# Two transformer-like layers on one core: one opening block with the loads that the first attention needs, the rest loaded and made during that attention

## What is computed

```
ga = (2 * (ga >= 0) - 1) * max(|ga|, 0.25)          # gb alike
h = layernorm(x) * (1 + ca) + sa ;  x = x + ga * attn(h)
h = layernorm(x) * (1 + cb) + sb ;  x = x + gb * ffn(h)
```

## Time and profile before

| | us |
|---|---|
| three runs | 4078.65, 4080.57, 4083.61 |
| median | 4080.57 |
| the profiled execution | 4077.96 |
| its span in the trace | 4076.2 |

### The profile page before, as it was taken

How to read it: one execution, slowest core, us unless ns; L and a number is a source line. 1 busy time by engine, 2 the same in 40 slices (tenths; PEclk the granted TensorE clock), 3 DMA queues, 4 the chain that set the end, 5 groups by cost and what they waited for, 6 DMA issues and landing times. The chain is left out here.

```text
span 4076.2 us, 49893 instructions
## 1 busy us (share of the span) xinstructions
PE 3502.1 (86%) x16757; PEld 2034.7 (50%) x16757; DVE 3318.9 (81%) x3665; ACT 2577.2 (63%) x3716; POOL 2721.2 (67%) x1957
## 2 busy tenths in 40 slices
PE   5488888989898998989897898989889898989876
PEld 3154553637355463736455373645546373644522
DVE  3513687989888898989887898988989898988997
ACT  2345666766676766766676676666667676667652
POOL 0031676958677685968766695877768696776892
PEclk9599999999999999999999999999999999999888
DMA  3520110303021020302112030301103030211100
GB/s 136 183 88 32 58 63 8 118 1 109 16 67 59 28 98 6 116 4 91 35 53 74 6 119 1 99 27 57 69 21 104 1 109 16 78 47 42 68 1 11
DMA packets 66249, 236.01 MB, mean 58 GB/s; under 512 B 9120, under 2 KB 9760, under 8 KB 65568
## 3 DMA queue, kind: packets, MB, share of 16 engines
q1 hardware_dynamic: 63648, 223.81, 16.3%
q10 hardware_dynamic: 2304, 8.39, 0.5%
HBM read 212.25 MB, written 19.92 MB: 57 GB/s over the span
## 5 line engine op out<-in xcount | busy, mean ns | idle before, releaser
L672 POOL TENSOR_TENSOR kept<-kept,hb 128x512 f32<-128x512 f32 x600 | 757.5, 1294 | 20.2 <-DVE hb L1989 19.6
L1980 DVE TENSOR_TENSOR_SCAN hb<-ps,hb 128x512 f32<-128x512 f32 x600 | 697.8, 1206 | 17.7 <-ACT ps L1404 13.1
L938 PE MATMUL ps<-hid_bhi,wring 128*128 128x512 f32 x1408 | 560.9, 398 | 16.0 <-DVE ln_s L2007 16.0
L938 PE MATMUL ps<-hid_blo,wring 128*128 128x512 f32 x1408 | 554.1, 394 | 0.0
L1404 ACT ACTIVATE ps<-kept,a_neg 128x512 f32<-128x512 f32 x600 | 403.3, 695 | 188.1 <-DVE hb L1980 188.1
L938 PE MATMUL ps<-hid_ahi,wring 128*128 128x512 f32 x1280 | 515.2, 402 | 4.9 <-DVE h_ln L2007 4.4
L633 POOL TENSOR_SCALAR_AFFINE_SELECT room<-room 128x512 f32<-128x512 f32 x256 | 224.3, 893 | 431.3 <-ACT room L1628 429.4
L938 PE MATMUL ps<-hid_alo,wring 128*128 128x512 f32 x1280 | 505.0, 395 | 0.0
L2055 DVE TENSOR_REDUCE room<-ps 128x4 f32<-128x2048 f32 (+3 forms) x256 | 375.1, 1486 | 118.1 <-PE ps L1132 118.1
L640 POOL TENSOR_TENSOR kept<-kept,hb 128x1024 f32<-128x1024 f32 x112 | 288.9, 2590 | 249.0 <-DVE hb L1924 181.1
L1628 ACT ACTIVATE room<-ps 128x2048 f32<-128x2048 f32 (+1 forms) x192 | 305.3, 1590 | 205.4 <-PE ps L1158 178.5
(11 more groups left out here) (319 smaller groups left out, 7680.1 us busy)
## 6 DMA issues: line engine op xcount, KB each, us to landing
wring<-w_hi SPq DMA_DIRECT2D x352, 512.0 KB, 3.3
kept<-in_wffn SPq DMA_DIRECT2D x22, 512.0 KB, 4.4
w_hi<-wring SPq DMA_DIRECT2D x22, 512.0 KB, 3.6
xn<-in_x_fm SPq DMA_DIRECT2D x17, 512.0 KB, 3.2
out_fm<-xc ACTq DMA_DIRECT2D x15, 512.0 KB, 2.7
room<-in_wmod SPq DMA_DIRECT2D x2, 1536.0 KB, 7.8
win<-in_win SPq DMA_DIRECT2D x1, 1024.0 KB, 8.7
wqk<-in_wqk SPq DMA_DIRECT2D x1, 512.0 KB, 5.7
```

What stands on the lines that cost most here:

```text
L672: pool.tensor_tensor(acc[:, m, :], acc[:, m, :], hb[:, s % 8, :], ALU.add).then_inc(acc_done, 1)
L938: mm = pe.matmul(bank(bk), w, x, start=(k == 0 and i == 0), stop=(k == K - 1 and i == 1))
L1980: dve.tensor_tensor_scan(hb[:, s % 8, :], bank(2 + m % 2), hb[:, s % 8, :], 0.0, ALU.mult, ALU.add).then_inc(scanned, 1)
```

## The change

The set-up block, the two small blocks and the layernorm pass become one block, `opening`. It issues 16 loads (both `c`, `mean_mat`, `x`, `wmod0`, and eleven more that the attention needs), has a semaphore for each of four groups of loads, and makes only layer 0's modulation, in the middle of which PE does the variance. The other 14 loads (3.9 MB; `wmod1` of 1536 KB, `win` of 1024 KB, `wout` of 512 KB, `ffw`, `wxp` and `wdt` of 256 KB each, and eight of 32 KB or less) are issued by SP in the first attention, one behind the load of each of the tiles 3 to 16. Layer 1's modulation and the state-space constants are made late in the first attention (`later_pe` behind `row_sums(1)`, `later_act` before `exp_probs(3, 1)`, `later_dve` behind `weigh(2)`). The rounding of the feed-forward weight goes to the start of the feed pass on DVE, its transposes and its copy to the end of that pass on PE and ACT. The calls `split` move two tiles ahead on ACT and DVE: tiles 0 and 1 come before the attention's first instruction, and each later place takes a tile two numbers higher.

```diff
-        with nc.Block() as block:
-            n_set = len(SETUP_LOADS) + 10
...
+        LATER = [(wxp, "wxp"), (wdt, "wdt"), (win, "win"), (s1, "s1"), (s2, "s2"), (sh1, "sh1"), (sh2, "sh2"),
+                 (ffb, "ffb"), (bdt_neg, "bdt"), (d_skip, "d_skip"), (wout, "wout")]
+        N_LATER = len(LATER) + 3
...
+        LATER_LOADS = [(wm[1], "wmod1"), (a_rows(), "a_log"), (ffw.rearrange("p a b -> p (a b)"), "ffw")] + [(whole(t), name) for t, name in LATER]
+
+        def modulation(pe, i, m, bk):
+            for c in range(DC):
+                mm = pe.matmul(bank(bk)[:, m * B:(m + 1) * B], wm[i][:, c, m * P:(m + 1) * P],
+                               c_s[:, i, c * B:(c + 1) * B], start=(c == 0), stop=(c == DC - 1))
+            return mm
...
+        def opening():
+            n_opening = 11
+            with nc.Block() as block:
+                @block.sync
+                def _(sp):
+                    sp.dma_start(c_in[:, 0, :], a["c0"]).then_inc(c_loaded, 16)
+                    sp.dma_start(c_in[:, 1, :], a["c1"]).then_inc(c_loaded, 16)
+                    sp.dma_start(whole(mean_mat), a["mean_mat"]).then_inc(x_loaded, 16)
+                    sp.dma_start(xn[:, :, :], a["x_fm"][0]).then_inc(x_loaded, 16)
+                    sp.dma_start(wm[0], a["wmod0"]).then_inc(mod_loaded, 16)
...
+                @block.scalar
+                def _(act):
+                    act.wait_ge(c_loaded, 32)
+                    act.activation(c_s, c_in, ACT.Silu).then_inc(set_act, 1)
+                    act.preload_act_table_set(LN_EXP)
+                    act.wait_ge(next_cent, 1)
+                    act.activation(qk_sq, ln_x[:, :, :], ACT.Square).then_inc(next_sq, 1)
+                    act.wait_ge(next_var_done, 1)
...
+                    act.wait_ge(set_pe, 1)
+                    copy_modulation(act, 0, 0)
+                    act.wait_ge(next_norm, 1)
+                    act.wait_ge(set_dve, 2)
...
+                @block.tensor
+                def _(pe):
+                    pe.wait_ge(x_loaded, 32)
+                    for c in range(DC):
+                        mm = pe.matmul(bank(6), mean_mat[:, :], xn[:, c, :], start=(c == 0), stop=(c == DC - 1))
+                    mm.then_inc(next_mean_done, 1)
+                    pe.wait_ge(mod_loaded, 16)
+                    pe.wait_ge(set_act, 1)
+                    for m in range(6 * DC):
+                        mm = modulation(pe, 0, m, 0)
+                        if m == 3:
+                            pe.wait_ge(next_sq, 1)
+                            for c in range(DC):
+                                vv = pe.matmul(bank(7), mean_mat[:, :], qk_sq[:, c, :], start=(c == 0), stop=(c == DC - 1))
+                            vv.then_inc(next_var_done, 1)
+                    mm.then_inc(set_pe, 1)
...
+                @block.vector
+                def _(dve):
+                    dve.wait_ge(next_mean_done, 1)
+                    dve.tensor_tensor(ln_x[:, :, :], xn[:, :, :], bcast_c(bank(6)), ALU.subtract).then_inc(next_cent, 1)
+                    dve.wait_ge(next_rstd_ready, 1)
+                    dve.tensor_tensor(ln_x[:, :, :], ln_x[:, :, :], bcast_c(bank(7)), ALU.mult).then_inc(next_norm, 1)
+                    dve.wait_ge(set_act, 2)
+                    scales_of(dve, 0)
+                    gates_of(dve, 0, 2)
+                    dve.wait_ge(loaded, 16 * n_opening)
...
+        def later_pe(pe):
+            pe.wait_ge(loaded, 16 * N_LATER)
+            for m in range(6 * DC):
+                mm = modulation(pe, 1, m, 5)
+            mm.then_inc(set_pe, 1)
+        def later_act(act):
+            act.wait_ge(loaded, 16 * N_LATER)
+            act.activation(a_rows(), a_rows(), ACT.Exp).then_inc(set_act, 1)
+            act.wait_ge(set_pe, 1)
+            copy_modulation(act, 1, 5)
+        def later_dve(dve):
+            dve.wait_ge(set_act, 2)
+            scales_of(dve, 1)
+            gates_of(dve, 1, 2)
...
+        def feed_dve(dve):
+            for i in range(QN):
+                quant(dve, ffw, DC * D // QB, set_dve, 12, i)
+        def feed_pe(pe):
+            pe.wait_ge(set_dve, 12 + QN)
...
                     sp.dma_start(stage[:, t % 3, :], a["wffn"][t]).then_inc(stage_loaded[t % 3], 16)
+                    if 3 <= t < 3 + N_LATER:
+                        to, name = LATER_LOADS[t - 3]
+                        sp.dma_start(to, a[name]).then_inc(loaded, 16)
...
             row_sums(1)
+            if first:
+                later_pe(pe)
             head_spread(0, 1)
...
+            split(0, 1)
             square(0)
...
             odd_version(0)
-            split(0)
+            split(2)
...
+            split(0, 1)
+            if ffn and not att:
+                feed_dve(dve)
             normalise(0)
...
         has_rest = None
-        run([Pass(-1, False, False, False, False, True, False, ())])
+        opening()
         turn_over()
```

More of the change, by code:

```diff
@@ L296, in quant @@
             ins.then_inc(own, 1)
-        c_t = part(REST + 0, DC, B)
-        c_s = part(REST + 64, 2, DC * B)
-        wm = [part(REST + 2560 + i * DC * 6 * D, DC, 6 * D) for i in range(2)]
         c_in = part(REST + 128, 2, DC * B)
-        a_log = part(REST + 256, IM * NS)
+        c_s = part(6144, 2, DC * B)
+        wm = [part(REST + 2560, DC, 6 * D), part(3072, DC, 6 * D)]
+        tmp_g = part(6208, 2 * 2 * DC * B)
         qk_in = part(REST + 384, 4)
@@ L307, in build @@
         grp = part(REST + 400, DC * 2 * D // HS)
-        ffw = part(REST + 1024, DC * D // QB, QB)
-        tmp_g = part(REST + 1536, 2 * 2 * DC * B)
         sel_in = part(REST + 2048, 2 * NS)
-        SETUP_LOADS = [(ident, "ident"), (mean_mat, "mean_mat"), (head_mat, "head_mat"), (sum_sel, "sum_sel"), (wqk, "wqk"), (wv, "wv"), (wu, "wu"),
-                       (win, "win"), (wxp, "wxp"), (wdt, "wdt"), (wout, "wout"), (s1, "s1"), (s2, "s2"), (sh1, "sh1"),
-                       (sh2, "sh2"), (s3, "s3"), (ffb, "ffb"), (bdt_neg, "bdt"), (d_skip, "d_skip")]
+        ffw = b_rows.rearrange("p a b -> p (a b)")[:, 0:DC * D].rearrange("p (a b) -> p a b", b=QB)
@@ new lines, in feed_dve, with feed_act @@
+        def feed_dve(dve):
[3 more added lines that the diff above has]
+            pe.wait_ge(set_dve, 12 + QN)
+            rows = ffw.rearrange("p a b -> p (a b)")
+            for r in range(DC):
+                for c in range(DC):
+                    mm = pe.transpose(bank(2)[:, c * D + r * P:c * D + (r + 1) * P], rows[:, r * D + c * P:r * D + (c + 1) * P], ident[:, :])
+            mm.then_inc(set_pe, 1)
+        def feed_act(act):
+            act.wait_ge(set_pe, 2)
+            act.activation(wdq[:, :, :], bank(2).rearrange("p (c n) -> p c n", c=DC), ACT.Copy).then_inc(set_act, 1)
@@ L1754, in scalar_pass @@
             exp_probs(2, 0)
-            split(21)
             skip(2)
@@ L1770, in scalar_pass @@
             copy_out(2)
+            if first:
+                later_act(act)
             exp_probs(3, 1)
@@ L1859, in scalar_pass @@
             rotate_b()
+            if ffn and not att:
+                feed_act(act)
         def vector_pass(dve, p):
@@ L2123, in vector_pass @@
             find_max(0, 1)
-            split(1)
+            split(3)
             normalise(3)
-            split(2)
+            split(4)
             tail_out(0, 0)
@@ L2189, in vector_pass @@
             weigh(2)
+            if first:
+                later_dve(dve)
             quant_at(1, 4, 5, 6, 7, 8, 9, 10, 11)
```

216 lines of the change are left out of this document (91 added, 125 removed).

## The result

The changed kernel takes 4058.67 us (median of five runs, 4055.03 to 4060.87) against 4079.28 for the kernel before (five runs on the same chip, 4078.65 to 4083.61): a ratio of 0.9947, interval 0.9933 to 0.9960. The forecast was 4064.5, range 4051 to 4073. The profiled execution after took 4057.48, span 4055.7: 20.5 us less than the one before, where the sum of the terms had said 16.2.

What follows compares the result with a forecast made beforehand. Chains bound the opening, a load-rounding-subtraction loop the first attention, later its dependences. Terms -35.7 + 1.0 - 0.3 + 2.0 + 9.5 + 0.3 + 7.0 = -16.2 us took the profiled 4077.96 to 4061.8, written 4064.5 as median; range 4051 to 4073.

Steps and rivals of the forecast that it cites:

- The opening: Set-up to the first attention: one block ends at 29.0 us instead of 64.74, -35.7 us, within 2 us either way.
- the rival's price of 6.3: Fast clock: PE goes fast behind the opening's mean and holds; opening 6.3 us better, total 4052.5; chance 0.21.
- Early tiles and loads: First attention: two tiles split ahead cost +1.0 us (0 to 1.8), later loads in SP's queue +2.0 (0 to 4.1).
- The rival of a loop that pays for every load: First attention: each of 14 loads holds the next tile back 3.5 us, 49 us instead of 2.0; 4111; chance 0.05.
- nothing hidden: Whole change: all moved work may stand on the path, 34.1 against 35.7 us, so -1.6, 4079; chance 0.09.
- The later modulation: Attention's tail on PE: 48 instructions of 8.6 us, 1.3 of it free, plus 2.2 for slower products: +9.5 us.
- The middle case: Later modulation: a third of its instructions fast, the rest slow, +9.5 us; 3.9 if the clock holds, 14 if all slow.
- The feed: Start of the feed pass: rounding delays DVE's centring, +5.2 us, and slows PE's variance, +1.8; together +7.0 (5.2 to 8).

Runs made afterwards that it cites:

- mod_in_gap: Changed kernel with layer 1's modulation on PE moved from the attention's tail to behind `scores_turned(0, 0)`, `wmod1` with its own semaphore: 4048.54 us, ratio 0.9923.
- mod_twice: Changed kernel with layer 1's modulation issued twice in the attention's tail, 96 instructions instead of 48: 4070.25 us in one run.
- both_in_gap: Changed kernel with layer 1's modulation behind `scores_turned(0, 0)` and the feed-forward rounding behind `split(6, 7, 8)`: 4046.49 us, ratio 0.9913.
- before_both: Kernel before with the splits two tiles ahead and the 14 loads issued once more in the first attention: 4080.77 us in one run.

## Why the prediction was right

**The opening** came out term by term: block end 28.8 (forecast 29.0), variance at 13.09 (12.9, where the terms 9.3 + 3.4 give 12.7), the 32 instructions at 0.214 us each. What held the kernel before, the landing of every load, then one engine at a time, was read rightly off.

**But it is not the only opening that occurs.** The forecast argued from 20 us at the slow pace that the clock would not rise, and gave the rise to a rival. Seven of the experiments ran the changed opening or a reordered one with nothing ahead of the mean; with the changed kernel that is eight traces. PE stayed slow to the end of the modulation in three, was fast for the last 32 instructions in three (3.99 to 4.05 us), and rose within the mean or right behind it in two. In these five the first DMA went out 2.7 to 4.9 us earlier than in the changed kernel's trace, more than the 2 us that the forecast allowed the opening; that the trace of the changed kernel is one of the three is luck. So that step of the argument failed: the row it rests on holds where the modulation is PE's first work, in five of five traces, and not behind a mean. The Trainium skill's page "TensorE: Matmul & The Clock Gate" (section "Part 1: The HAM clock gate") says that the point of the rise differs from run to run of one kernel; these traces agree. The Trainium skill's general rule there, that sustained matmul activity releases the throttle, fails at the kernel before: 20.6 us of the modulation never did.

It matters less than the rival's price of 6.3. In the traces whose first DMA went out 2.7 to 2.9 us earlier than after with the same loads (mod_in_gap, mod_twice, both_in_gap) the first exponential came at 82.63, 81.85 and 81.63, against 82.34 and 81.78 in the two with a slow opening. In those three the clock was back at 0.50 in the attention's products 28 to 40 us behind the first DMA, DVE's maxima and the measures of tiles behind them came later, and with them the loads: the one that goes out 40.5 us behind the first DMA in the changed kernel went out at 41.5 to 41.7. Most of the gain was given back, in mod_twice too, which differs from the changed kernel by nothing up to there. This chain is read from the traces; no run set the clock to try it.

**Early tiles and loads.** The two terms, 1.0 and 2.0, measured about 1 at the attention's start and 0.5 to 2 at the first exponential, but they do not simply add up there: the trace pair shows +1.2 for both, against the second trace of the kernel before it is nothing, and before_both, at a lower clock, shows 2.0 and 3.2 against the two. So 3.0 was within what occurs and too much for the profiled execution; that its slow first products hid the early tiles is part of the reason, the rest is open. The rival of a loop that pays for every load (49 us) is out: 14 loads in the kernel before left its end where it was, 4078.49. So is "nothing hidden".

**The later modulation.** +9.5 was forecast and +9.1 measured, out of two errors that cancel: its length was 6.37 and not 8.6, because the clock held for the first 4.3 us of it, and the slow tail behind it cost some 4 and not 2.2 (9.1 less 6.37 - 1.3). The middle case was the right one: the clock fell inside the block, 2.6 to 4.3 us behind its start in all five traces that have it there; in eight of the nine without it the clock stayed at 1.00 for 13 us or more behind the start of `row_sums(1)`. Where the 48 stand there once they took 6.37 to 7.87 us, and the stretch 35.3 each time. The first trace of the kernel before was a short one in this stretch, 26.3 where seven other tails without the modulation took 27.9 and one 29.7; against the seven the modulation cost 7.4, and moving it gave 7.5 there and 8.5 at the end.

**The feed.** +7.0 against +6.9: 5.1 us for the rounding on DVE and 1.8 for the slow variance. The first is shown, since it goes when the rounding goes. For the second the reason given, an idle stretch, is half of it. In all five traces with the rounding in the feed the variance took 3.37 to 3.75. In four of them the mean ahead of it was fast (1.95 or 1.96) and the clock fell in the 6.8 us of idle time between the two, as forecast; in the changed kernel's own trace it had fallen before the mean (3.75). With 1.7 us of idle time the variance took 1.95 or 1.96 in the six traces whose mean was fast, and 3.71 to 3.75 in the three whose mean was slow already (2.56 to 3.75).

**What the sum did not have** is 2.2 us less behind the feed's first product. 1.1 of it lies in the feed's products: the clock rises some 3 us into them in the changed kernel and some 5 us in the kernel before. The rest lies between pass 1's first projection and the end, 3744.7 us instead of 3745.9, and stays unexplained. Neither part recurs: from the feed's first product to the projection the other thirteen traces took 91.7 to 91.9 us, this one 90.7; behind it twelve of them took 3745.9 to 3746.7, mod_twice 3749.6. So nothing shows that these 2.2 us come with the change.

So the forecast lay 5.8 us above the median with every large term right, and the range held it. Of the 5.8, 1.3 is the median before (4080.57 of three runs, 4079.28 of five), 1.8 the early tiles and loads, and 2.2 the end of that one trace.

## What to carry to other kernels

Ask of every piece that a change moves what its new neighbour waits for: two pieces here landed where their engine had nothing to hide them, and one call each, put into waits of 14 us (PE) and 12 us (DVE) that the profile shows, gave 12.7 us more (20.6 became 33.3), and a reordered opening brought it to 39.2. Where a term hangs on the clock of TensorE, take a second trace of the unchanged kernel before explaining 1 us: the same code differed by 1.2 us at one instruction. A gain ahead of a loop that is bound by something else may arrive there only in part, as in three traces here.

## What the runs showed of the hardware that was not expected

The 128x16 fp32 modulation runs at 0.215 us an instruction for 20.6 us without raising the clock (five of five traces), and at a granted 1.00 it didn't keep it in the attention's tail: the clock fell to 0.50 between 2.6 and 4.3 us into the block, in five of five traces, with PE busy without a gap. Behind a mean of four 128x512 instructions the same instructions ran at 0.12 to 0.135 us, all or the last 32 of them, in five of eight traces. One order of work thus has several lengths, and in this kernel a stretch that ends 3 us sooner can meet a slower clock in the next.
